# A mixture-of-experts tail in pairs: the last 26 tiles as 8 single tiles and 9 pairs, first product as three fp32r products of 256 columns

## The reference

```python
gate_logits = xs @ Wg
weights, sel = jax.lax.top_k(gate_logits, TOP_K)
weights = jax.nn.softmax(weights.astype(jnp.float32), axis=1).astype(x.dtype)
h = jax.nn.relu(jnp.einsum('td,edf->etf', xs, W1) + b1[:, None, :])
out_e = jnp.einsum('etf,efd->etd', h, W2) + b2[:, None, :]
picked = out_e[sel, tok[:, None]]
out = jnp.einsum('tk,tkd->td', weights, picked)
```

## Time and profile before

| What | us |
|---|---|
| time, median of 3 runs | 622.43 (621.24 to 622.68) |
| time of the profiled execution | 621.19 |
| its span, first to last instruction | 619.5 |
| PE (TensorE matmul) busy | 558.3 (90%) |
| VectorE busy | 358.3 (58%) |
| ScalarE busy | 330.6 (53%) |
| POOL busy | 233.8 (38%) |
| granted TensorE clock, mean over the span | 0.956 |

### The profile page before, as it was taken

The page is one execution under the profiler, slowest core; times in us unless marked ns, Lnnn a source line. Parts: engine busy times, 40 slices in busy tenths (PEclk is TensorE's granted clock), DMA queues, the critical chain, the costliest instruction groups (busy, mean ns, idle before and its releaser), DMA issues.

```text
span 619.5 us, 15514 instructions
## 1 busy us (share of the span) xinstructions
PE 558.3 (90%) x5075; PEld 483.4 (78%) x5076; DVE 358.3 (58%) x841; ACT 330.6 (53%) x726; POOL 233.8 (38%) x301
## 2 busy tenths in 40 slices
PE   3767989999999999978966899999999999999991
PEld 3755767777777767655545899999999999999991
DVE  3647776969687886867657786573233233233230
ACT  4532367564655665524643944555655655655650
POOL 7423222223241320200435544426446455455432
PEclk9878999999999999986995999999999999999996
DMA  8474744443719090751267856657667667667641
GB/s 226 129 124 107 80 69 53 76 82 55 102 34 124 13 139 10 108 124 62 95 228 224 275 162 171 179 168 225 197 175 229 191 177 225 190 184 226 183 95 17
DMA packets 56008, 85.71 MB, mean 138 GB/s; under 512 B 6672, under 2 KB 44720, under 8 KB 55952
## 3 DMA queue, kind: packets, MB, share of 16 engines
q1 hardware_dynamic: 46368, 73.59, 46.9%
q0 software_dynamic: 7872, 10.33, 8.9%
q10 hardware_dynamic: 1712, 1.05, 0.6%
HBM read 62.44 MB, written 9.31 MB: 116 GB/s over the span
## 4 chain that ended last, share of the span: by engine, by line
PE 41%; DMA 30%; DVE 9%; issue 7%; ACT 6%; SPq 2%; POOLq 1%; POOL 1%; DVEq 0%; ACTq 0%
DMA out<-y,scatter_now 27%; PE bank L1220 13%; PE pair L1467 5%; PE bank L1606 4%; PE pair L1571 4%; PE pair L2357 4%; PE pair L1502 2%; PE bank L2397 2%; DVE row_max L1514 2%; SPq L1543 2%; DMA q_stack<-max_lo 2%; PE bank L1181 2%; DMA exp_ring<-L_attn_Wo 1%; PE bank L1701 1%; ACT exp_ring L1588 1%
## 5 line engine op out<-in xcount | busy, mean ns | idle before, releaser
L2357 PE MATMUL pair<-slots_t,w_now 128*128 128x128 f32 x1248 | 146.9, 276 | 0.0
L2357 PEld LDWEIGHTS pair<-slots_t,w_now 128*128 128x128 f32 x1248 | 143.6, 193 | 0.0
L2367 ACT ACTIVATE hid<-pair,b_tile 128x128 f32<-128x128 f32 x312 | 88.6, 367 | 53.9 <-PE pair L2357 49.5
L2377 DVE TENSOR_TENSOR hid_lo<-hid,hid_hi 128x1024 fp32r<-128x1024 f32 x39 | 47.9, 1227 | 105.5 <-ACT hid_hi L2374 99.5
L2310 POOL DMA_INDIRECT out<-y,scatter_now x39 | 64.3, 1649 | 113.0 <-DMA out<-y,scatter_now 75.3
L1514 DVE TENSOR_REDUCE row_max<-pair 128x4 f32<-128x1024 f32 x64 | 78.1, 1222 | 23.0 <-PE pair L1502 23.0
L2397 PE MATMUL bank<-experts_w,hid_hi 128*128 x624 | 82.5, 284 | 0.0
L1588 ACT ACTIVATE exp_ring<-pair 128x1024 f32<-128x1024 f32 x64 | 64.9, 1028 | 27.3 <-PE pair L1571 24.0
L2397 PEld LDWEIGHTS bank<-experts_w,hid_hi 128*128 128x128 f32 x624 | 75.7, 188 | 0.0
L2295 POOL DMA_INDIRECT slots_in<-xn_rows,gather_now x39 | 43.1, 1105 | 25.9 <-POOL gather_now L2292 15.5
L2374 ACT ACTIVATE hid_hi<-hid 128x512 fp32r<-128x512 f32 x78 | 49.3, 632 | 4.7
(11 more groups left out here) (295 smaller groups left out, 1075.9 us busy)
## 6 DMA issues: line engine op xcount, KB each, us to landing
w_now<-L_ffn_W SPq DMA_DIRECT2D x39, 1024.0 KB
experts_w<-L_ffn_W SPq DMA_DIRECT2D x8, 1024.0 KB, 7.2
k_stack<-ck_hi SPq DMA_DIRECT2D x32, 128.0 KB, 4.3
q_stack<-cq_hi SPq DMA_DIRECT2D x32, 128.0 KB, 4.4
ctx_in<-ctx SPq DMA_DIRECT2D x8, 256.0 KB, 2.7
k_stack<-ck_lo SPq DMA_DIRECT2D x16, 128.0 KB, 5.4
q_stack<-cq_lo SPq DMA_DIRECT2D x16, 128.0 KB, 5.1
out<-x SPq DMA_DIRECT2D x7, 256.0 KB, 5.0
```

Of the source, the lines that this page charges most:

```text
L2357: mm = eng.matmul(banks[half][:, f * P:(f + 1) * P], core.w1_now[b.p][:, c, start:start + P], core.slots_t[b.p][:, c, :], start=c == 0, st ...
L2367: act = eng.activation(core.hid[:, g, :], banks[half][:, f * P:(f + 1) * P], ACT.Relu, bias=core.b1_tile[b.p][:, g:g + 1])
L2377: core.m["hid_lo"].at(eng.tensor_tensor(core.hid_lo[b.p][:, :, :], core.hid[:, :, :], core.hid_hi[b.p][:, :, :].bitcast(F32), ALU.subtract))
```

## The change

The tiles are 39 as before. Tiles 0 to 20 stay single tiles; the last 18 become 9 pairs, each of two tiles of one expert. `last_tiles` fills the tables for 8 single tiles (13 to 20) and for the 9 pairs; it has more steps, since it counts pairs, running sums included, once more. The hardware loop is gone: everything is written out.

A pair loads W1 once instead of twice, in two halves of 512 columns (512 KB each, runs of 2 KB). There is one buffer for it: half h of a pair is loaded when TensorE has done half h of the hidden product of the pair before. ScalarE rounds the half to fp32r (`w1_hi`), VectorE subtracts in place to get `w1_lo`. The 256 rows of the pair are turned by four transposes, ScalarE rounds them (`x_hi`), VectorE subtracts (`x_lo`). The hidden product of a half is 4 blocks x 3 terms x 2 halves of the contraction, 24 instructions of 256 columns. The second product is 24 instructions of 256 columns for a half, 48 for a pair as before.

The core of the diff (left out: the renaming of a semaphore group, table sizes, small helpers, the removal of `pipeline`, and the new arguments of `tile_numbers`):

```diff
-LAST = MAX_TILES + 1 - FIRST
+LAST = MAX_TILES - FIRST
+ODD = NE
+SINGLES = FIRST + ODD
+PAIR_SLOTS = (LAST - ODD + 1) // 2
+assert SINGLES + 2 * PAIR_SLOTS == MAX_TILES
+UNIT = FT // 2
 PARTS = (slice(0, TA), slice(TA, TT))
 LOCAL = (TA, TT)
...
     w1_odd = sb("w1_now1", [KT, FF])
+    core.cursor = start
+    core.w1_lo = sb("w1_lo", [KT, FF], F32R)
     core.hid_lo = [sb(f"hid_lo{i}", [FT, P], F32R) for i in range(2)]
     end, core.cursor = core.cursor, core.x2_at
     core.w1_now = [sb("w1_now0", [KT, FF]), w1_odd]
+    core.cursor = core.x2_at
+    core.w1_hi = sb("w1_hi", [KT, FF], F32R)
     core.hid = sb("hid", [FT, P])
     assert core.cursor <= core.x2_at + EARLY_BATCHES * KT * D * 4
+    core.cursor = core.x2_at + EARLY_BATCHES * KT * D * 4
+    core.x_lo = sb("x_lo", [KT, 2 * P], F32R)
+    assert core.cursor <= core.x2_at + TT * D * 4
     core.cursor = start
     core.row_hot = ([sb(f"row_hot{i}", [count(0), P], F32R) for i in range(2)], [row_hot])
     core.tile_vals = ([sb(f"tile_vals{i}", [count(0), 3, *col_shape(0)], F32R) for i in range(2)], [tile_vals])
@@ -477,7 +482,8 @@
...
+    link(core, name, e.tensor_tensor(core.alone[:, :], core.own_tiles[:, :], core.taken[:, :], ALU.subtract))
+    settle(core, name, e)
+    link(core, name, e.scalar_tensor_tensor(out=core.cmp_count[:, :, 0:NE], in0=bc(core.alone[:, :], [P, NE, NE], 2),
+                                      scalar=0.5, in1=bc(core.iota_f[:, 1:NE + 1], [P, NE, NE], 1),
+                                      op0=ALU.mult, op1=ALU.is_ge))
+    settle(core, name, e)
+    link(core, name, e.tensor_reduce(core.tiles_of[0][:, :], core.cmp_count[:, :, 0:NE], AX.X, ALU.add))
+    settle(core, name, e)
     ends = running_sum(core, name, e, [b[:, :] for b in core.tiles_of], NE)
-    tile_numbers(core, name, e, ends, LAST)
-    link(core, name, e.scalar_tensor_tensor(out=core.col_f[:, :], in0=core.col_f[:, :], scalar=core.taken[:, 0:1],
-                                      in1=core.iota_f[:, 0:LAST], op0=ALU.add, op1=ALU.add))
-    settle(core, name, e)
+    link(core, name, e.tensor_scalar(core.pairs_to[:, :], ends, float(PAIR_SLOTS), 2.0, ALU.min, ALU.mult))
+    settle(core, name, e)
...
+    for part, upto, first, done in ((slice(0, ODD), ends, core.singles_at, core.own_tiles),
+                                    (slice(ODD, LAST), core.pairs_to, core.taken, core.singles_at)):
+        n = part.stop - part.start
+        link(core, name, e.tensor_tensor(core.jump[:, 0:NE - 1], first[:, 1:], done[:, 0:NE - 1], ALU.subtract))
+        settle(core, name, e)
+        link(core, name, e.tensor_scalar(core.jump[:, 0:NE - 1], core.jump[:, 0:NE - 1], float(LOCAL[1]), None, ALU.add))
+        settle(core, name, e)
+        tile_numbers(core, name, e, upto, part, NE)
+        link(core, name, e.scalar_tensor_tensor(out=core.col_f[:, part], in0=core.col_f[:, part], scalar=first[:, 0:1],
+                                          in1=core.iota_f[:, 0:n], op0=ALU.add, op1=ALU.add))
+        settle(core, name, e)
...
+def experts_sync_order(core, eng):
+    singles(core, "sync", eng, range(SINGLES))
+    for q in range(PAIR_SLOTS):
+        for half in range(2):
+            pair_load(core, eng, q, half)
...
+def experts_gpsimd(core, eng):
+    singles(core, "gpsimd", eng, range(SINGLES))
+    for j in range(2):
+        pair_gather(core, eng, 0, j)
+        singles(core, "gpsimd", eng, [SINGLES + j])
+    for j in range(2):
+        pair_gather(core, eng, 1, j)
+        singles(core, "gpsimd", eng, [SINGLES + 2 + j])
+    for q in range(PAIR_SLOTS):
+        for j in range(2):
+            if q + 2 < PAIR_SLOTS:
+                pair_gather(core, eng, q + 2, j)
+            ex_scatter(core, "gpsimd", eng, unit(q, j))
...
+def experts_tensor(core, eng):
+    singles(core, "tensor", eng, range(SINGLES + 1))
+    last_single(core, "tensor", eng, ex_hidden)
+    pair_rows_tensor(core, eng, 0)
+    ex_out(core, "tensor", eng, tile(SINGLES - 2))
+    for q in range(PAIR_SLOTS):
+        pair_hidden_tensor(core, eng, q, 0)
+        if q == 0:
+            last_single(core, "tensor", eng, ex_out)
+        else:
+            pair_out_tensor(core, eng, q - 1, 1)
+        pair_hidden_tensor(core, eng, q, 1)
+        if q + 1 < PAIR_SLOTS:
+            pair_rows_tensor(core, eng, q + 1)
+        pair_out_tensor(core, eng, q, 0)
+    pair_out_tensor(core, eng, PAIR_SLOTS - 1, 1)
...
+def experts_scalar(core, eng):
+    singles(core, "scalar", eng, range(SINGLES + 1))
+    last_single(core, "scalar", eng, ex_hidden)
+    pair_rows_scalar(core, eng, 0)
+    pair_round_scalar(core, eng, 0, 0)
+    for q in range(PAIR_SLOTS):
+        pair_round_scalar(core, eng, q, 1)
+        pair_relu_scalar(core, eng, q, 0, 0)
+        pair_high_scalar(core, eng, q, 0, 0)
+        pair_relu_scalar(core, eng, q, 0, 1)
+        pair_high_scalar(core, eng, q, 0, 1)
+        if q + 1 < PAIR_SLOTS:
+            pair_round_scalar(core, eng, q + 1, 0)
+        pair_relu_scalar(core, eng, q, 1, 0)
+        pair_high_scalar(core, eng, q, 1, 0)
+        pair_relu_scalar(core, eng, q, 1, 1)
+        if q + 1 < PAIR_SLOTS:
+            pair_rows_scalar(core, eng, q + 1)
+        pair_high_scalar(core, eng, q, 1, 1)
...
+def experts_vector(core, eng):
+    singles(core, "vector", eng, range(SINGLES + 1))
+    last_single(core, "vector", eng, ex_hidden)
+    pair_bias_vector(core, eng, 0)
+    pair_rows_vector(core, eng, 0)
+    pair_rest_vector(core, eng, 0, 0)
+    ex_out(core, "vector", eng, tile(SINGLES - 2))
+    for q in range(PAIR_SLOTS):
+        pair_rest_vector(core, eng, q, 1)
+        pair_low_vector(core, eng, q, 0)
+        if q == 0:
+            last_single(core, "vector", eng, ex_out)
+        else:
+            pair_out_vector(core, eng, q - 1)
+        if q + 1 < PAIR_SLOTS:
+            pair_bias_vector(core, eng, q + 1)
+            pair_rest_vector(core, eng, q + 1, 0)
+            pair_rows_vector(core, eng, q + 1)
+        pair_low_vector(core, eng, q, 1)
+    pair_out_vector(core, eng, PAIR_SLOTS - 1)
...
+def pair_load(core, eng, q, half):
+    core.m["hid"].wait(eng, unit(q, half).back(2))
+    x = pair_expert(core, eng, q)
+    rows = core.t["L0_ffn_W1"].rearrange("e (k p) n -> p e k n", p=P)
+    cols = half_columns(half)
+    core.w1_in.at(eng.dma_start(core.w1_now[1][:, :, cols].rearrange("p (e k) n -> p e k n", e=1),
+                                rows[:, bass.ds(x * -1 + (NE - 1), 1), :, cols]), unit(q, half))
...
+def pair_gather(core, eng, q, j):
+    b = unit(q, j)
+    rows, now = pair_buffer(core, q, j)
+    core.rows_in.wait(eng, b.back(2))
+    if q == 1:
+        core.m["xT"].wait(eng, tile(SINGLES - 1))
+    elif q > 1:
+        core.m["xT"].wait(eng, pair_step(q - 2))
+    g, col = column_of(core, eng, b)
+    core.m["gnow"].at(eng.tensor_copy(now[:, :], core.gather_idx[g][:, bass.ds(col, 1)]))
+    core.m["gnow"].wait(eng, b)
+    core.rows_in.at(eng.indirect_dma_start(
+        rows[:, :], None, core.xn_dram[0:PARTS[g].stop * P, :],
+        bass.IndirectOffsetOnAxis(ap=now[:, :], axis=0)), b)
...
+def pair_rows_tensor(core, eng, q):
+    for j in range(2):
+        core.rows_in.wait(eng, unit(q, j))
+    core.m["slots_t"].wait(eng, pair_step(q - 1))
+    if q > 0:
+        eng.wait_ge(core.x_rest, q)
+    for c in range(KT):
+        for j in range(2):
+            mm = eng.transpose(core.psum[0][:, c * 2 * P + j * P:c * 2 * P + (j + 1) * P],
+                               pair_buffer(core, q, j)[0][:, c * P:(c + 1) * P], core.ident[:, :])
+    core.m["xT"].at(mm)
...
+def pair_rows_scalar(core, eng, q):
+    core.m["xT"].wait(eng, pair_step(q))
+    core.m["hid"].wait(eng, unit(q, 0).back(1))
+    core.m["slots_t"].at(eng.activation(core.x_hi[:, :, :], core.psum[0][:, :], ACT.Copy))
...
+def pair_rows_vector(core, eng, q):
+    core.m["slots_t"].wait(eng, pair_step(q))
+    if q == 0:
+        eng.wait_ge(core.E["residual_out"], 16 * (NB - EARLY_BATCHES))
+    else:
+        core.m["hid"].wait(eng, unit(q - 1, 1))
+    eng.tensor_tensor(core.x_lo[:, :, :], core.psum[0][:, :], core.x_hi[:, :, :].bitcast(F32), ALU.subtract)        .then_inc(core.x_rest, 1)
...
+def pair_round_scalar(core, eng, q, half):
+    core.w1_in.wait(eng, unit(q, half))
+    if q == 0:
+        core.m["hid"].wait(eng, tile(SINGLES - 1), half)
+    else:
+        core.m["hid"].wait(eng, unit(q - 1, half))
+    cols = half_columns(half)
+    eng.activation(core.w1_hi[:, :, cols], core.w1_now[1][:, :, cols], ACT.Copy).then_inc(core.split["hi"], 1)
...
+def pair_rest_vector(core, eng, q, half):
+    eng.wait_ge(core.split["hi"], NE + 2 * q + half + 1)
+    cols = half_columns(half)
+    eng.tensor_tensor(core.w1_lo[:, :, cols], core.w1_now[1][:, :, cols],
+                      core.w1_hi[:, :, cols].bitcast(F32), ALU.subtract).then_inc(core.split["lo"], 1)
...
+def pair_hidden_tensor(core, eng, q, half):
+    u = unit(q, half)
+    bank = core.pair[u.p]
+    if half == 0:
```

(103 more changed lines are left out.)

74 lines of the change are left out of this document (45 added, 29 removed).

## The result

The changed kernel takes 680.9 us in the median of four runs (679.4 to 682.9), the kernel before 621.8 beside it: ratio 1.0955, interval 1.0918 to 1.0992. Forecast were 614 and a range of 610 to 620.5. The change makes the kernel 9.5% slower.

What follows compares the result with a forecast made beforehand. TensorE was taken as the bound, scatters close behind. Stream -13.6, loop of waits +2.6, joint +2.4 and tables +1.0 summed to -7.6 from 621.2, so 613.6, written as 614; range 610 to 620.5.

Steps and rivals of the forecast that it cites:

- At no cost: Rows fetched two pairs ahead, POOL's four indirect DMAs a pair, row copies, the end and unrolled code: nothing added.
- The rival on scatters: Scatters on POOL's queue set the pairs' pace at 6.6 each, 13.2 a pair: 623.2, no change; chance 0.08.
- TensorE's stream: TensorE's products and transposes for a pair take 11.67 instead of 13.20, at 0.117 a product; term -13.6.
- The loop of waits: W1's single buffer: load, ScalarE rounding and product loop 11.6, as long as TensorE's stream; period 12.0, +2.6 for eight.
- rival on late loads: W1 half landing above 3.8 lengthens the period; at 5.4, 626.4, chance 0.08; half way, 617 to 620.4, chance 0.12.
- The joint: Where single tiles give way to pairs, TensorE waits for the first pair's rounding and W1 remainder: about +2.4.
- The tables: Longer `last_tiles` on VectorE, about 7.7, delays scatter 8 and tile 13's gather; TensorE waits 1.0, between 0.5 and 2.
- the 0.5 for the signal: In the tables' term, time left between tile 13's last gather packet and TensorE's use; an estimate between 0 and 1.
- The end: The kernel's tail after the last products: as before, two scatters one behind the other, no added cost.
- the 1.2 added: In the final sum, the median of before lies 1.2 above its profiled execution, so 613.6 was written as 614.

Runs made afterwards that it cites:

- gathers_early: Changed kernel with gathers of pair q+3, not q+2, ahead of the scatters of pair q, and single tiles' gathers from tile 13 one scatter earlier: 617.7, ratio 0.9938.
- short_scatters: The changed kernel with pair q+3's gathers ahead of pair q's scatters, and scatters of pairs 1 to 7 writing 8 of 128 rows: 618.3, one run.

## Why the prediction was wrong

**The step that failed** stands under "At no cost": "The tiles' rows come two pairs ahead. POOL has four indirect DMAs a pair as before". The count was right; what stands ahead of each in the queue was not looked at. The rows come two pairs ahead in number, but the second gather of q+2 is issued behind the scatter of q, whose y comes late in the turn of q+1. The parts of the 8.85 could be had from rows ahead of the change: y's operations, the copy, the scatter and the gather behind it, a landing of 2.9 or more. Against 2.8 of first product they leave a hole of 3 or more (an estimate from these rows), seven times. The rival on scatters spoke of their rate, not of what is queued behind them. The order of GpSimd's queue alone takes 49 of the 59 back.

**What the hole does to the clock** had no term at all: 12.8 in the pairs' second products, and 1.6 behind tile 13's hole. The 4.2 in the transposes behind a hole had none either.

**TensorE's stream** was right: 11.67 forecast, 11.69 to 11.70 measured where nothing is waited for, 0.117 a product.

**The loop of waits** was near in its parts, with the landing 3.8 where 3.4 stood. By the forecast's own sum the loop is then 12.0, and by its rival on late loads the period stays at 12.0 up to that landing; measured are 12.38 and 11.98 in the two kernels that keep the forecast's order on ScalarE (gathers_early, short_scatters), and 11.99 to 12.02 in the three where `x_hi` comes sooner. The path from a scatter's landing through y's buffer was not in the sum, and how much of the period it makes stays open. In the changed kernel this loop is covered by the longer one.

**The joint** was forecast at 2.4 and took 1.8: 0.35 ahead of the first product and 1.44 in its first half, behind the remainder of W1. The 1.0 in the same turn, ahead of the second pair's transposes, is a wait for rows again: they start 4.69 behind the issue of their second gather (499.70 to 504.39). That both together come near 2.4 is chance.

**The tables** were mis-sized: forecast 1.0, measured 5.6. `last_tiles` took 8.2 (408.53 to 416.69), forecast 7.7. But the scatter behind the late y took 2.42 to issue instead of 1.59, the gather came at 426.53 and its rows were taken 5.25 later, where 2.9 and 0.5 were counted (the 0.5 for the signal stands on no row), and the clock added 1.6. The DMA engines were 0.81 busy meanwhile, at 289 GB/s.

**The end** was put at nothing ("two scatters one behind the other") and costs 3.0: there are four.

With the order of the gathers mended the forecast's mechanism holds, though not its size: 0.9938 is 3.9 faster, not 7.6. As far as the traces tell, the end (3.0) takes most of the difference, and the first pair's transposes wait 1.5 for their rows there. The forecast's own sum, with the 1.2 added, is 614.8 and not 614; nothing hangs on it.

## What to carry to other kernels

When work is grouped in pairs, redo the distances in every in-order queue in units of the new group: for each transfer that is fetched ahead, ask what stands before it in its queue, what that waits for, and how long before the need this comes. A prefetch distance of two means nothing behind a store that waits for the current result; in this kernel moving the gathers ahead of the scatters, one pair further, and those of the single tiles one scatter ahead, turned 9.5% slower into 0.6% faster. Count the tail of a serial chain of stores once more too: results that come in groups leave in single file.
